# Two 3x3 convolutions at the end of a windowed-attention block: operands laid out as four columns in the partitions, placed by DMA, and half taps on half of the array

## The reference

```
xr = short_cut + project(attention(q, k, v))
y  = xr + conv3(gelu(conv3(xr, c1w, c1b)), c2w, c2b)
out = x + y
```

## Time and profile before

| | |
|---|---|
| median of 3 runs | 833.27 us (832.16 to 835.34) |
| profiled execution: its time | 835.37 us |
| profiled execution: its span | 833.5 us |
| TensorE busy | 753.8 us (90%) |
| VectorE, ScalarE, GpSimd busy | 656.3 (79%), 603.4 (72%), 491.1 us (59%) |
| DMA packets of the kernel's queue | 46.09 MB, 16.1% of 16 engines' span |
| granted TensorE clock, mean | 0.988 of full speed |

### The profile page before, as it was taken

One profiled execution on the slowest core, in us unless ns is written; L12 is line 12 of the kernel. 1 busy time (PEld: TensorE's weight loads), 2 busy tenths in 40 slices (PEclk: granted clock), 3 DMA queues, 4 the chain that ended last, 5 costly groups with the idle time before them and its releaser, 6 DMA issues.

```text
span 833.5 us, 18393 instructions
## 1 busy us (share of the span) xinstructions
PE 753.8 (90%) x5704; PEld 538.0 (65%) x5704; DVE 656.3 (79%) x2141; ACT 603.4 (72%) x1287; POOL 491.1 (59%) x1041
## 2 busy tenths in 40 slices
PE   0479999989899999999899999998989999999988
PEld 0347777767456777777556677776745677776753
DVE  6548888879768888888757888887877888887575
ACT  1488888876577888876747888877757788887750
POOL 5447776763356777765246776776235677776410
PEclk9989999999999999999899999999999999999999
DMA  7101160000112142100111216100011303000002
GB/s 255 57 29 29 31 230 22 36 2 1 58 64 94 31 135 96 58 2 1 58 39 52 70 30 230 57 2 1 2 57 64 96 30 130 0 1 1 2 1 101
DMA packets 17643, 47.00 MB, mean 56 GB/s; under 512 B 2080, under 2 KB 2720, under 8 KB 17568
## 3 DMA queue, kind: packets, MB, share of 16 engines
q1 hardware_dynamic: 17568, 46.09, 16.1%
HBM read 37.69 MB, written 8.39 MB: 55 GB/s over the span
## 4 chain that ended last, share of the span: by engine, by line
PE 47%; DVE 18%; issue 12%; ACT 11%; POOL 10%; DVEq 0%; DMA 0%; SPq 0%; ACTq 0%; POOLq 0%
PE y_ps L1013 12%; PE o_bank L1092 5%; PE s_ps L1067 4%; PE pt_ps L1080 4%; POOL ln_rs L724 4%; DVE ln_st L542 3%; ACT qk_n L858 3%; PE s_ps L1126 3%; PE ox_ps L1036 3%; PE ox_ps L1126 3%; PE o_bank L1126 3%; PE pt_ps L1126 3%; DVE pt L584 2%; PE t_ps L1047 2%; ACT sc L873 2%
## 5 line engine op out<-in xcount | busy, mean ns | idle before, releaser
L858 ACT ACTIVATE qk_n<-y_ps,ln_nr,ln_rs 128x128 f32<-128x128 f32 x256 | 103.7, 459 | 84.7 <-POOL ln_nr L727 84.0
L737 POOL TENSOR_TENSOR sc<-sc,mx 128x512 f32<-128x512 f32 x128 | 133.7, 1045 | 37.8 <-DVE mx L577 37.4
L1013 PE MATMUL y_ps<-w_hi,x_hi 128*128 128x192 f16 (+1 forms) x512 | 150.1, 293 | 0.0
L1013 PE MATMUL y_ps<-w_lo,x_hi 128*128 128x192 f16 (+1 forms) x512 | 149.6, 292 | 0.0
L1013 PE MATMUL y_ps<-w_hi,x_lo 128*128 128x192 f16 (+1 forms) x512 | 149.5, 292 | 0.0
L1092 PE MATMUL o_bank<-v_bd,pt 128*128 128x66 f32 x1024 | 128.6, 268 | 0.0
L562 DVE TENSOR_TENSOR sc<-s_ps,biasS 128x512 f32<-128x512 f32 x128 | 86.8, 678 | 50.3 <-PE s_ps L1067 49.0
L542 DVE BATCH_NORM_STATS2 ln_st<-y_ps 128x6 f32<-128x128 f32 x384 | 88.9, 287 | 45.6 <-PE y_ps L1013 43.9
L1092 PEld LDWEIGHTS o_bank<-v_bd,pt 128*128 128x128 f32 x1024 | 124.5, 192 | 0.2
L724 POOL TENSOR_TENSOR ln_rs<-ln_ve,neg_half 128x3 f32<-128x3 f32 x128 | 113.0, 883 | 10.7
L873 ACT ACTIVATE sc<-sc 128x512 f32<-128x512 f32 x128 | 81.5, 636 | 39.4 <-POOL sc L737 39.3
(11 more groups left out here) (181 smaller groups left out, 1614.6 us busy)
## 6 DMA issues: line engine op xcount, KB each, us to landing
xs<-in_x_sh_dram SPq DMA_DIRECT2D x32, 576.0 KB, 4.2
xst<-in_x_al_dram SPq DMA_DIRECT2D x16, 512.0 KB, 8.0
xf<-in_x_al_dram SPq DMA_DIRECT2D x32, 256.0 KB, 5.4
out_dram<-xf SPq DMA_DIRECT2D x32, 256.0 KB, 2.0
wst<-in_wqkv_dram SPq DMA_DIRECT2D x1, 768.0 KB, 4.1
w1s<-in_w_dram SPq DMA_DIRECT2D x1, 256.0 KB, 8.7
w2s<-in_w_dram SPq DMA_DIRECT2D x1, 256.0 KB, 8.7
biasS<-in_bias_t_dram SPq DMA_DIRECT2D x1, 256.0 KB, 9.5
```

The source lines that it names most:

```text
L737: pool.tensor_tensor(sc[i % 4][:, :, :, :], sc[i % 4][:, :, :, :], mx[i % 2][:, :, :].unsqueeze(2).to_broadcast([P, HP, TOK, 2]), ALU.subt ...
L858: ins = act.activation(qk_n[j][:, t, :].rearrange("p (h y x) -> p h y x", h=HEADS, y=2), by_head(y_ps[j][:, E * t:E * (t + 1)]), ACT.Identity,
L1013: ins = pe.matmul(y.rearrange("p (t e) -> p t e", t=3)[:, :, cols], xx[r % 2][:, s, a % 2, 2 * TS * (a // 2):2 * TS * (a // 2 + TS)], ww[: ...
```

## The change

**Layout.** Both convolutions now read one tile `x4` [128, 2, 2, 66, 66]. A partition is (`ax`, column parity, channel), that is four neighbouring columns of 32 channels; row parity and the split part are in the free dimension. Each value stands twice in `x4`, once for `ax` = 0 and once, a block column further left, for `ax` = 1. The first convolution's input and its output after gelu share `x4`: rows of `h` overwrite rows of `xr`.

**How it gets there.** The engines write the splits into small buffers, `xr_st` (2, for bands of 8 rows) and `h_st` (4, for tiles of 5 rows), and SyncE's queue copies each with four DMAs of 64 partitions (row parity x `ax`) into `x4`. A copy of a band is 64 x 2 x 528 fp16 elements (135 KB), of a tile of h 64 x 2 x 330 (84 KB). Per image these are 8 x 4 + 13 x 4 = 84 DMAs. `ax` = 1 reads its source one element (2 bytes) further on. TensorE waits for the landing (`x_in`, `h_in`), where before it waited for the writer.

**Borders.** `low` now clears the two outer columns of its own tile, four memsets of 32 partitions x 10 elements, before the tile is copied; `border` is gone.

**Matmuls.** A tile is still 12 matmuls over the same columns, four vertical taps `k` by three products. Two of the four taps (1 and 2 in c1, 0 and 3 in c2) have full 128x128 weights. Of the other two, the half of the output columns whose weights are zero is left out: each is a matmul with 64 weight columns, one into partitions 0 to 63 and the next into 64 to 127, in turn.

**Order.** c1 tiles 11 and 12 stand behind c2 tile 0 in the seam (in the tail they stand ahead of it, as before). Two banks of c2 change places. A c2 tile waits only for the tiles of h that it reads.

```diff
+            def place_x(b, r):
+                sp.wait_ge(xr_split, b * NROW + (r + 1))
+                for py in range(2):
+                    for ax in range(2):
+                        src = xr_st[r % 2][64 * py:64 * py + 64, :, :, :].rearrange("p l i j -> p l (i j)")
+                        dst = x4[64 * ax:64 * ax + 64, :, py, :, :].rearrange("p l i j -> p l (i j)")
+                        at = (TS * r + 1) * (G + 2)
+                        sp.dma_start(dst[:, :, at:at + TS * (G + 2) - ax], src[:, :, ax:TS * (G + 2)]).then_inc(
+                            x_in[r % 2], 16)
...
                     load_image(b + 1)
-                    for r in range(4):
+                    for r in range(2):
                         row(b + 1, r)
+                for r in range(6):
+                    place_x(b, r)
+                for t in range(4):
+                    place_h(b, t)
+                place_x(b, 6)
+                for t in range(4, 6):
+                    place_h(b, t)
+                if followed:
+                    for r in range(2, 4):
+                        row(b + 1, r)
+                place_x(b, 7)
+                for t in range(6, T1N):
+                    place_h(b, t)
...
             def low(b, t):
...
+                n = b * T1N + t
+                hs = h_st[n % 4]
+                v.wait_ge(gelu_done, n + 1)
+                if n >= 4:
+                    v.wait_ge(h_in[n % 4], 64 * (n // 4))
+                v.tensor_scalar(hs[:, 0, :, 0:G + 1], hst[t % 6][:, :, :], up[:, 1:2], None, ALU.mult).then_inc(
                     h_hi_done, 1)
...
+                v.wait_ge(h_split, n + 1)
+                for q in range(4):
+                    out_of = 0 if q % 2 else G
+                    ins = v.memset(hs[32 * q:32 * q + 32, :, :, out_of:out_of + 1], 0.0)
+                ins.then_inc(h_clean, 1)
...
-                pe.wait_ge(xr_split, b * NROW + min((T1R * (t + 1) - 1) // TS, NROW - 1) + 1)
+                k = min((T1R * (t + 1) - 1) // TS, NROW - 1)
+                pe.wait_ge(x_in[k % 2], 64 * (b * (NROW // 2) + k // 2 + 1))
...
-                for a in range(4):
-                    ay, ax = a // 2, a % 2
-                    for n, (ww, xx) in enumerate(((w1_hi, xr_hi), (w1_hi, xr_lo), (w1_lo, xr_hi))):
-                        ins = pe.matmul(c1_bank[t][:, 0:T1R * (G + 1)], ww[:, a, :],
-                                        xx[:, T1R * t + ay:T1R * (t + 1) + ay, ax:ax + G + 1],
-                                        start=(a == 0 and n == 0), stop=(a == 3 and n == 2))
+                def tap(k, ww, l, m, **ends):
+                    return pe.matmul(c1_bank[t][m, 0:T1R * (G + 1)], ww[:, k, m],
+                                     x4[:, l, k % 2, T1R * t + k // 2:T1R * (t + 1) + k // 2, 0:G + 1], **ends)
+
+                for n, (ww, l) in enumerate(((w1_hi, 0), (w1_hi, 1), (w1_lo, 0))):
+                    for k in (1, 2):
+                        tap(k, ww, l, slice(0, P), start=(n == 0 and k == 1), stop=False)
+                for n, (ww, l) in enumerate(((w1_hi, 0), (w1_hi, 1), (w1_lo, 0))):
+                    tap(0, ww, l, slice(P // 2, P), start=False, stop=(n == 2))
+                    ins = tap(3, ww, l, slice(0, P // 2), start=False, stop=(n == 2))
```

129 lines of the change are left out of this document (69 added, 60 removed).

## The result

The changed kernel takes 873.62 us (median of 4 executions, 871.46 to 876.21), the kernel before 833.03 on the same chip: ratio 1.048, interval 1.047 to 1.050. The forecast was 840 with a range to 853: right that it is slower, 34 us short of how much, and outside the range of 821 to 853.

The account below looks back on a forecast made before the run. TensorE bounds the seam from the next image's first convolution on, and c2 in the tail. 833.5 + 3 x 0 + 6.4 = 839.9 of span, so 840 us; range 821 to 853.

Parts of the forecast that it names:

- part 1: TensorE's convolution tiles: a pair of halves takes one slot; c1 saves 0.12 us a tile, c2 0.36.
- The switch: TensorE going in and out of the halved array, once a tile: 0.30 us, bounds 0 or no pairing.
- rival on the halves: TensorE's half matmuls: free switch, 827 us, chance 0.32; or halves one after another, 865 us, chance 0.10.
- part 2: VectorE's h tiles: four more memsets add 0.80 us a tile, so xn_aff comes 4.8 later.
- part 3: SyncE's copies: bands 0 to 5 hidden, band 6 lands at 215.5 and c1 tile 9 waits for it.
- 0.33 + 3 x 0.49 = 1.8 to issue: SyncE's four copies of a band or h tile: 1.8 us to issue, landed at 3.35.
- the copies are slow: Rival on SyncE's queue: 1.0 us a copy instead of 0.45, about 880 us, chance 0.10.
- part 4: Seam between images: 1.9 us lost by c2 tile 1, 2.2 given back by six c2 tiles, 0.3 for statistics.
- Net per seam: 0: Sum for each of three seams between images: no time gained or lost.
- part 5: Last image and tail: 7.1 us lost behind late bands 6 and 7, 0.7 saved by six c1 tiles, together +6.4.
- Nothing for the rest: GpSimd's zeroing at the start and the later loads of window rows 2 and 3: no cost.

Follow-up runs that it names:

- e1: Kernel before with two of four taps of both convolutions computed for half the output columns, no copies or memsets (output not the block's): 821.28 us, ratio 0.986.
- e8: Changed kernel without the four border memsets of each h tile: 871.42 us, ratio 1.046.
- e13: e12 with ScalarE's x_hi copies of the next image's row 1 ahead of the gelu of c1 tiles 11 and 12: 833.78 us, ratio 1.001.
- e16: e13 with side columns zeroed by a mask multiplication on GpSimd instead of VectorE's four memsets: 829.77 us, ratio 0.995.
- e14: e13 with VectorE's low part of h tile 3 moved behind the normalised output of the last attention pair: 837.19 us, ratio 1.004.
- e15: e14 with side columns zeroed by a mask multiplication on GpSimd instead of VectorE's four memsets: 828.34 us, ratio 0.994.
- e4: Changed kernel with ScalarE's x_hi copies of the next image's row 1 ahead of the gelu of c1 tiles 11 and 12: 865.34 us, ratio 1.038.
- e6: e5 with e4's order, x_hi of the next image's row 1 ahead of the gelu of c1 tiles 11 and 12: 853.43 us, ratio 1.023.
- e3: Changed kernel with the copies of bands 6 and 7 issued by ScalarE instead of SyncE: 874.83 us, ratio 1.050.
- e5: e3 with SyncE's loads of the next image's rows 2 and 3 moved behind h tile 9: 863.25 us, ratio 1.036.
- e2: Changed kernel with all four taps on all 128 output columns, copies and memsets kept: 883.82 us, ratio 1.060.
- e12: Changed kernel with c1 as in the kernel before, no band copies, only c2 in the new layout, row loads behind h tile 9: 846.99 us, ratio 1.017.
- e9: e6 with the four border memsets of each h tile replaced by one mask multiplication on VectorE: 854.14 us, ratio 1.023.

## Why the prediction was wrong

**The matmuls (part 1): right.** Pairs of halves share a slot. The switch was put at 0.30 a tile and is 0.24: by twelve slots of 0.219 becoming nine, 2.63 should become 1.97; it became 2.06, with 0.15 more on the transposes behind. The saving was put at 0.36 and is 0.42 for c2, 0.12 and 0.16 for c1. The Trainium skill (TensorEngine Tiling (Array Packing), Key Properties) has a drain at a change of tiling mode, and e1 agrees with a cost there of that size (2.09 for nine slots of 0.219, and 0.37 for the transposes). Neither rival on the halves came true.

**VectorE (part 2): right in size, wrong in what it costs.** A tile takes 1.76 us (201.98 to 203.74) where it took 0.90: +0.86, +0.80 forecast; 0.17 of it is the high part, 0.56 instead of 0.39; the one thing that changed in that instruction is that the 65 elements of a row are now written 66 apart instead of one row behind the other. From the first `low` to `xn_aff` it is 11.5 us instead of 7.3: +4.2, 4.8 forecast. In the changed kernel the copies cover the memsets (e8: 2 us). In the kernel without band copies, taking them off VectorE gave 4.0 us (e13 to e16), or 8.9 where e14's order had made it worse (e14 to e15).

**SyncE's queue (part 3): the mechanism right, the term that failed first.** "0.33 + 3 x 0.49 = 1.8 to issue": an issue takes 0.61 and the next starts 0.65 after it, so a tile takes 2.6, and it is the same for copies of 82 and of 132 KB. At 1.8 a tile the queue would have kept up with VectorE's 1.76; at 2.6 it falls behind by 0.8 a tile. The sixteen copies are out at 214.1 where 212.2 was forecast, although the first tile was ready 0.7 us sooner than forecast, and band 6 takes 4.9 us from its first issue to its last landing where 3.35 was forecast: 1.9 + 1.6 = 3.5, and so c1 tile 9 starts at 219.07 instead of 215.5. The landing of one copy was priced well: 2.2 for an h tile, 2.5 for a band, 2.0 forecast. The rival "the copies are slow" had this at 1.0 us a copy and gave 880: the right mechanism at a price too high, and the rest of the time came from elsewhere.

**One seam (part 4): "Net per seam: 0" is the step that failed most**, 8.2, 10.0 and 8.6 us, 27 of the 39. Two reasons. The sum followed TensorE and band 7 only, and there the 3.5 us of band 6 came back enlarged: the clock at 0.50 made c1 tile 9 2.7 us long instead of 2.2 and the projection 2.1 instead of 1.3, the four copies of band 7, like those of band 6, took longer than 3.35 (4.5 us), and c1 tile 11 started at 231.2 instead of 225.5. And it left out a path: gelu of tiles 11 and 12, `x_hi` of row 1, `x_lo`, `ln_ve` stand one behind the other on ScalarE and GpSimd, and so the next image's first layer norm waits for the very last c1 tile. e4, e6 and e13 price it at 8, 10 and 7 to 13 us. I had followed the moved c1 tiles on TensorE, and not their gelu on ScalarE.

**The tail (part 5): right in mechanism, half in size.** +6.4 forecast with 7.1 lost in the tail, 13.4 measured there: band 6 lands 834.35 - 817.66 = 16.7 after the first `low` where 12.8 was forecast, band 7 11.9 behind it where 9.6 was forecast; c2 then runs as forecast, eight tiles of 2.17.

**"Nothing for the rest"** was wrong on the row loads in e3: there they filled the DMA engines in front of band 7, and moving them gave 11.6 us (e5). In the changed kernel they stand ahead of band 7 too, but it was issued 0.03 us after its split, and its copies landed 2.4 to 2.6 us after their issue in seam 1 and at most 3.1 in the others. So little of its time can be theirs; moving them there was not tried alone.

What the change costs and gives is then, in medians: halves -12 (e1); everything that the layout needs, +51 (with the 10.2 of e2); without the band copies and with the row loads late 847.0 (e12), with `x_hi` first 833.8 (e13), with the mask off VectorE 829.8 (e16) or 828.3 (e15). Above e1's 821.3 this leaves 7 to 8 us for h copies, the longer low part and c1's full taps, which no run takes apart. By the table 4.5 of them lie in the tail (-2.3 in e1, 2.2 in e16), where c2 waits for its copies.

## What to carry to other kernels

A layout that needs copies inside the chip is paid for at the place where its last copy is late, so ask of each consumer separately whether it can wait. Here c1, which gained 0.16 us a tile from the layout, lost some 27 us by it (873.6 to 847.0, the later row loads included; 21 to 33 over the executions of e12). c2 alone was still slower than the kernel before; after two repairs in other places, `x_hi` first and the mask on GpSimd, it is 4 to 5 us faster, and waits for its copies in the tail. When a step is moved or made late, follow it through every in-order engine that its result passes, not only through the one on which the time was lost. And a cost that measures 2 us in the shadow of another (e8) can be 4 once the other is gone (e13 to e16): measure it again after each repair. Before you set a time of one run beside that of another, take off how far apart the two already were: 1.4 of the 3.5 us that `xn_aff` seems to gain in e15 were there before the seam.

## What was not expected of the hardware

- A copy of 64 partitions from one place of the chip's memory to another took SyncE 0.59 to 0.61 us to issue in a line, 0.65 from one to the next, whether of 82 or 132 KB and hardly less in 64 pieces than in 128 (0.597 and 0.607 in the median; the shortest went from 0.59 to 0.46); a store of 256 KB had taken 0.33.
- Such a line kept the 16 DMA engines at 0.60 of their time. A second queue beside it brought them to 0.93 to 1.10 with the row loads (e3), and the landing of a band's copy from 2.5 to between 2.5 and 7.8 us; without the row loads near it the landing was 2.4 to 4.5 (e5). The Trainium skill (SBUF — State Buffer, Door 1) gives 196 GB/s for 64 partitions, measured at 1 MiB; as an estimate from that page a band's copy would take 0.69 and an h tile's 0.43. Here both stood 0.65 apart. For a band that is near the page's figure, for an h tile it is not, so it is not the bytes that set the distance between the h copies.
- One multiplication of two columns on VectorE (0.22 us as a rule, up to 1.05) was cheaper than four memsets (0.48 together) and gained nothing, as VectorE then waited for the copies (e9); on GpSimd, ahead of the low part and on fp32, it took 0.20 us and was worth 4 us (e13 to e16).
